# A kernel of eight layers on one core: in the last attention the value products of a quad of heads move one step later, behind the turning of row maxima, and sums and output products follow

## The reference, cut to what matters

```python
def _L3_ffn_ref(x, router_prob, norm_w, norm_b, q_w, q_b, k_w, k_b, v_w, v_b, o_w, o_b):
    ...
    for e in range(e_cnt):                    # e_cnt = 4 quarters of n = 64 tokens
        xn = _layernorm(x[:, e * n:(e + 1) * n, :], norm_w, norm_b)
        m = d // 2 ** e
        xm = xn[..., :m]
        qs.append(jnp.einsum('bnm,dm->bnd', xm, q_w[:, :m]) + q_b)
        ...                                   # k and v in the same way
    attn = jnp.einsum('bhqd,bhkd->bhqk', q, k) * scale
    attn = jax.nn.softmax(attn, axis=-1)
    attn_out = jnp.einsum('bhqk,bhkd->bhqd', attn, v)
    ...                                       # output projection of each quarter, + x
```

## Time and profile before

| | us |
|---|---|
| median of 3 runs (lowest, highest) | 2036.42 (2035.14, 2037.17) |
| the profiled execution | 2036.34 |
| its span, first to last instruction | 2034.6 |
| busy: PE, DVE, ACT, POOL | 1728.0, 1585.6, 1251.1, 348.9 |
| first matmul of the last attention | 1911.52 |
| start of step 3, 8, 16, 24, 32 | 1923.34, 1936.27, 1960.35, 1984.44, 2004.37 |
| first matmul of the closing layer norm | 2021.79 |
| end of the span | 2034.6 |

### The profile page before, as it was taken

How to read it: one execution, slowest core, us unless ns; L and a number is a source line. 1 busy time by engine, 2 the same in 40 slices (tenths; PEclk the granted TensorE clock), 3 DMA queues, 4 the chain that set the end, 5 groups by cost and what they waited for, 6 DMA issues and landing times. The chain is left out here.

```text
span 2034.6 us, 46173 instructions
## 1 busy us (share of the span) xinstructions
PE 1728.0 (85%) x16491; PEld 1083.0 (53%) x16498; DVE 1585.6 (78%) x3793; ACT 1251.1 (61%) x3209; POOL 348.9 (17%) x464
## 2 busy tenths in 40 slices
PE   5999969846859999947759999999968999999585
PEld 5999944435633444425544444444436666665453
DVE  4444459878878999967878999999967787777774
ACT  5666637723526655555438888888856666665465
POOL 1000001000011111110001212222113443443211
PEclk7555569978968999978989999999979999999798
DMA  3000007210004443300006666666620000000100
GB/s 79 10 4 4 4 15 271 88 43 1 0 14 171 154 171 149 141 17 1 0 12 232 232 232 225 224 226 229 232 87 22 22 1 22 21 1 1 36 2 22
DMA packets 51670, 174.06 MB, mean 86 GB/s; under 512 B 7104, under 2 KB 32448, under 8 KB 34112
## 3 DMA queue, kind: packets, MB, share of 16 engines
q1 hardware_dynamic: 50368, 170.09, 23.3%
q10 hardware_dynamic: 1152, 1.90, 0.3%
HBM read 167.45 MB, written 2.95 MB: 84 GB/s over the span
## 5 line engine op out<-in xcount | busy, mean ns | idle before, releaser
L861 DVE TENSOR_TENSOR ps<-ps,m_comb 128x512 f32<-128x512 f32 x520 | 363.1, 699 | 23.9 <-DMA m_comb<-m_shares 7.2
L846 DVE TENSOR_TENSOR m_hwlo<-ps,m_hwhi 128x512 f16<-128x512 f32 x520 | 353.5, 680 | 0.3
L822 ACT ACTIVATE m_hwhi<-ps 128x512 f16<-128x512 f32 x520 | 308.3, 593 | 20.8 <-DVE ps L861 19.4
L828 ACT ACTIVATE ps<-ps 128x512 f32<-128x512 f32 x388 | 225.9, 582 | 80.7 <-PE ps L778 80.5
L778 PE MATMUL ps<-x_hi,m_whi 128*128 128x512 f16 x652 | 250.3, 384 | 8.2 <-DVE m_hwlo L846 4.2
L778 PE MATMUL ps<-x_lo,m_whi 128*128 128x512 f16 x652 | 250.0, 383 | 0.0
L778 PE MATMUL ps<-x_hi,m_wlo 128*128 128x512 f16 x652 | 249.7, 383 | 0.0
L759 POOL CAST m_whi<-m_stage 128x256 f16<-128x256 f32 (+1 forms) x130 | 55.2, 424 | 907.2 <-PE ps L784 637.6
L461 DVE TENSOR_TENSOR rn_s_lo<-rn_s_full,rn_s_hi 128x32 f16<-128x32 f32 x512 | 98.4, 192 | 131.5 <-ACT rn_s_full L418 131.5
L784 PE MATMUL ps<-m_hwhi,m_whi 128*128 128x512 f16 x520 | 197.4, 380 | 0.3 <-DVE m_hwlo L846 0.2
L784 PE MATMUL ps<-m_hwlo,m_whi 128*128 128x512 f16 x520 | 197.3, 379 | 0.0
(11 more groups left out here) (451 smaller groups left out, 3983.8 us busy)
## 6 DMA issues: line engine op xcount, KB each, us to landing
m_comb<-m_shares SPq DMA_DIRECT2D x128, 1024.0 KB, 5.1
m_stage<-in_m_w SPq DMA_DIRECT2D x97, 128.0 KB, 4.6
m_stage<-in_m_w SPq DMA_DIRECT2D x33, 192.0 KB, 4.7
lj_w<-in_lj_w SPq DMA_DIRECT2D x6, 1024.0 KB, 5.1
lq_w<-in_lq_w SPq DMA_DIRECT2D x1, 1600.0 KB, 6.9
la_w<-in_la_w SPq DMA_DIRECT2D x1, 1280.0 KB, 5.3
rn_rows<-in_L_attn_rows SPq DMA_DIRECT2D x4, 256.0 KB, 4.5
rn_xs<-rn_xn_hi SPq DMA_DIRECT2D x32, 32.0 KB, 1.9
```

Of the source, the lines that this page charges most:

```text
L822: nc.scalar.activation(hw_hi[:, k % HB, :], weighted(k), ACT.Copy).then_inc(hi_done, 1)
L828: nc.scalar.activation(acted(k), ps[:, 4, :] if gated else bank(k), func).then_inc(act_done, 1)
L846: nc.vector.tensor_tensor(hw_lo[:, k % HB, :], weighted(k), hw_hi[:, k % HB, :], ALU.subtract)\
L861: nc.vector.tensor_tensor(weighted(k), bank(k), comb[:, s, n * QW:(n + 1) * QW], ALU.mult)\
```

## The change

The value products go from lag 5 to lag 6 of a quad, which is an even step, where they stand behind the turning of the maxima in PE's list. Everything behind them goes one step later too: sums, logarithm, reciprocal and POOL's product from lag 8 to 9, rounding and rest from 9 to 10, output products and DVE's addition from 10 to 11. `STEPS` grows by one. The fills stay where they are. No instruction is added or taken out, and no bank changes.

```diff
-        STEPS = PAIRS + 12
+        STEPS = PAIRS + 13
...
 @block.tensor
-                if (b := batch(s, 8)) is not None:
+                if (b := batch(s, 9)) is not None:
                     pe.wait_ge(u_on, 2 * b + 2)
                     claim(6, logs_s, b + 1)
...
-                if (n := quad(s, 5)) is not None:
+                if (n := quad(s, 6)) is not None:
                     b, a = n // HG, n % HG
                     pe.wait_ge(exp_s, 2 * n + 2)
                     pe.wait_ge(v_s, b + 1)
...
-                if (b := batch(s, 10)) is not None:
+                if (b := batch(s, 11)) is not None:
                     pe.wait_ge(o_lo_s, b + 1)
                     claim(7, y_on, b + 1)
...
 @block.scalar
-                if (n := quad(s, 5)) is not None:
+                if (n := quad(s, 6)) is not None:
                     act.wait_ge(u_up, n + 1)
...
-                if (b := batch(s, 8)) is not None:
+                if (b := batch(s, 9)) is not None:
                     act.wait_ge(sums_up, b + 1)
...
-                if (b := batch(s, 9)) is not None:
+                if (b := batch(s, 10)) is not None:
                     act.wait_ge(o_s, b + 1)
...
 @block.gpsimd
-                if (b := batch(s, 8)) is not None:
+                if (b := batch(s, 9)) is not None:
                     pool.wait_ge(rec_s, b + 1)
...
-                if (b := batch(s, 9)) is not None:
+                if (b := batch(s, 10)) is not None:
                     pool.wait_ge(o_hi_s, b + 1)
...
 @block.vector
-                if (b := batch(s, 10)) is not None:
+                if (b := batch(s, 11)) is not None:
                     cut = slice(b * T, (b + 1) * T)
```

## The result

| | us |
|---|---|
| before, median of 20 runs (lowest, highest) | 2036.88 (2033.97, 2043.11) |
| changed, median of 20 runs (lowest, highest) | 2040.41 (2037.41, 2044.83) |
| ratio changed / before, 95% interval | 1.0016 (1.0008 to 1.0023) |
| the profiled execution of the changed kernel, its span | 2043.37, 2041.5 |

The change costs 3.3 us (0.16% of 2036.4; the interval is 1.6 to 4.7), where 0.9 was forecast. The changed kernel's times also scatter more: 11 of the 20 lie above 2039.9, of the 20 of before two do.

What follows compares the result with a forecast made beforehand. A step-to-step chain was taken to bind, no engine being full. Steps 4 to 7 and cycles (-0.56, -0.63, -0.28, +0.27) plus tail (+2.1) gave +0.9, so 2037.3 us; own range 2035.5 to 2038.8, 8-in-10 range 2034.6 to 2040.2.

Steps and rivals of the forecast that it cites:

- Cycles: Steps 4 to 7 9.96 us (before 10.52), cycles with fills 23.45 and 23.81 (24.08, 24.09), without fills 20.20 (19.93).
- The wait for the logarithm: Odd steps with sums and a fill: the fill waits on bank 6 for the sums' logarithm, step takes 3.63 us.
- the late release of bank 6 in step 11: Step 3 of a cycle: q fill waits for the k fill, released at 1.75 us; the step takes 2.96.
- the short even steps: Even steps: value products partly hidden under the chain's 2.50 us; steps take 2.50 to 2.92.
- the first step of a cycle: Step 0 of a cycle: value products wait for bank 7, DVE having other work ahead; 2.86 us.
- the even steps of the last cycle: Cycle without fills: the reciprocal ends a little after the next exponential is due, making the even step 2.58 us.
- Tail: From the start of step 32, last value products start at +10.4 us instead of +8.31, costing +2.1.
- the queue that was named: Tail: the last quad's value products wait behind batch 6's output products, on PE and on bank 7.
- Sum at full clock: Whole change: -0.56 - 0.63 - 0.28 + 0.27 + 2.1 = +0.9 us.
- the half clock in the tail: Rival: PE's 2.4 us idle behind quad 14 drops its clock in the tail, +2.7 us, 2040.0; chance 0.12.
- a sign of its being wrong: Listed as showing the forecast wrong: a TensorE clock below 1 before the last sums.
- The rival without a collision: Sums and fill don't collide in steps 9, 13, 17, 21: 2.71 us each, not 3.63; 3.7 less, 2033.6; chance 0.08.

Runs made afterwards that it cites:

- the last quad first: Changed kernel with the last quad's value products one step earlier, ahead of batch 6's output products; median 2037.51 us, ratio to before 1.0004.
- the fills through bank 7: Changed kernel with the fills of steps 1 and 5 of a cycle through bank 7 instead of bank 6; median 2041.79 us, ratio to before 1.0025.
- the tail of its own: Changed kernel with the last quad's value products and last sums ahead of batch 6's output products, no extra matmuls; median 2034.5 us, ratio to before 0.9995.

## Why the prediction was right in its order and wrong in its size

- **Cycles.** Forecast 9.96, 23.45, 23.81 and 20.20; measured 10.01, 23.40, 23.66 and 19.94 (with the clock at 1.00). The wait for the logarithm, the late release of bank 6 in step 11 and the short even steps all came as replayed, no step off by more than 0.11. The forecast of -1.2 became -1.6 by two small terms: the first step of a cycle, put at 2.86, took 2.76 and 2.75, and the even steps of the last cycle were put at 2.58. Steps 26 and 30 took 2.50 instead, since the reciprocal held the exponential no longer than the chain allowed.
- **Tail.** Forecast +10.4, measured +10.38, by the queue that was named; running the last quad ahead of it took the wait away.
- **Sum at full clock.** -1.6 and +2.1 are +0.5; forecast +0.9.
- **The step that failed** is the one in which I gave the half clock in the tail a chance of 0.12, on the ground that the clock of before had stood through waits of 1.09 and 0.61, and with it the sentence that from the last value products on each operation follows as before. In all three profiles of the changed kernel the clock fell before the last sums, which stood in the prediction as a sign of its being wrong. The cheap form costs 1.3 on top of the order's 0.5; the other form, in one of three, begins in step 32 and costs 6.3. The rival's price of 2.7 lies between the two and its test (a clock below 1 at the last value products) is what the profiles show, but its cause was drawn too narrow: I blamed the 2.4 us gap behind quad 14. In the late form the output products right behind that gap still ran at full clock (0.20 for the first at 2013.09, as in the earlier trace rows), and in the early fall no gap since step 24 had been longer than 0.97 us. What makes the clock fall earlier than before in this order stays open; that it goes with the new order rests on three profiles out of three against none out of two, and on the variants: of those in the new order without extra matmuls, the last quad first and the fills through bank 7 fell before the sums too, the tail of its own did not.
- **The rival without a collision** was right to be given little. The experiment with bank 7 shows that taking the wait away brings no gain, because the value products of the next step then wait for the fill's copy behind ACT's queue.
- **The bounds.** The ratio put on the median of the three runs gives 2036.42 x 1.0016 = 2039.7, inside 2034.6 to 2040.2 but above the forecast's own range of 2035.5 to 2038.8; the plain median of the later set, 2040.41, lies just above the end, beside a before that was 0.5 higher too. No change within 0.2% was right as a verdict, and slower by a little was the truth. There is luck in it: the range reached up to 2040.2 only because it took in a rival with a chance of 0.12, and the median lies there as a mixture of short and long executions whose share nothing in the prediction gave.

## What to carry to other kernels

Before moving work one step later in a hand-ordered pipeline, replay one cycle from the durations and waits of the trace, and then the drain: the cycle here gained 1.6 us, and the drain, where nothing covers a delay, gave back 2.1. Look then at what the new order does to the matmul engine's idle gaps near the end, because a fall of its clock can cost more than the whole move; a few matmuls that nobody reads, and a profile with them, are a cheap test of that. In the drain, let the last block's work stand ahead of the block before it where it waits only for its own inputs; here that took 3.0 off the way from step 32 to the last value products (7.37 for 10.38).

## What the runs showed of the hardware that was not expected

The clock of TensorE fell from 2.4 to 1.2 GHz after nothing but short gaps: in the first profile of the changed kernel PE was busy 0.33 and 0.69 of the two microseconds from 2001 on and without a gap from 2003 to the fall, with the longest gap 0.97 us. The same gap of 0.97 stands in the same place, before the output products of step 31, in the two other profiles of this kernel (2003.39 and 2000.56), which kept their clock there. The first of the two microseconds:

```profile
2001.00:2002.00 1.00, 0.33 (x10) 0.05 (x2) 0.86 (x1) 0.65 (x2) 0.90 (x1) 1.00 0.00 0
```

Two profiles of the same program with the same cycles fell at different places, step 32 and the last value products (some 10 us apart), which is worth 5 us of time. In the early form it did not come back to 2.4 GHz in the 23 us to the last output products, although PE was then busy without a gap for stretches of several microseconds (4.00 of the 4 from 2006 to 2010, though a matmul's end is modelled in these rows):

```profile
2006.00:2010.00 4.00, 4.00 (x22) 1.54 (x18) 0.00 (x0) 1.41 (x2) 0.00 (x0) 0.50 0.02 4
```

What decides between the early and the late fall was not found; three profiles are too few for a share.
